# Two PSUM banks in turn instead of one for the broadcast of the q and k norms

## What is computed

```
xn  = layernorm(x)                                  # x: 4 x 4096 x 1024, f32
qkv = xn @ w_qkv;  q, k, v of 16 heads of 64
qn  = q / max(norm(q), 1e-12);  kn = k / max(norm(k), 1e-12)
att = softmax(qn @ kn.T * exp(min(logit_scale, log 100))) @ v;   att @ w_out + b_out
ffn = relu(xn @ quant(W1).T + b1) @ quant(W2).T + b2  # quant: to -1, 0, 1
out = x + attention(xn) + ffn(xn)
```

## Time and profile before

| | us |
|---|---|
| runs of the kernel before | 7316.56 and 7632.47 |
| their median | 7474.52 |
| the profiled execution, its own time | 7146.77 |
| its span (slowest core, core 2), first to last instruction | 7144.7 |
| spans of all cores | 7095.8 to 7144.7 |
| mean granted TensorE clock of the cores | 0.902 to 0.905 |
| TensorE busy with matmuls | 5821.0 (81%) |
| ScalarE busy | 2882.6 (40%) |
| VectorE busy | 2340.2 (33%) |
| mean DMA rate over the span | 78 GB/s |

### The profile page before, as it was taken

The page is one execution under the profiler, slowest core; times in us unless marked ns, Lnnn a source line. Parts: engine busy times, 40 slices in busy tenths (PEclk is TensorE's granted clock), DMA queues, the critical chain, the costliest instruction groups (busy, mean ns, idle before and its releaser), DMA issues.

```text
span 7144.7 us, 70041 instructions; the slowest of 8 cores (7095.8 to 7144.7 us)
## 1 busy us (share of the span) xinstructions
PE 5821.0 (81%) x23681; PEld 2005.4 (28%) x24072; DVE 2340.2 (33%) x2493; ACT 2882.6 (40%) x3080; POOL 21.4 (0%) x44
## 2 busy tenths in 40 slices
PE   0577877888587898889888989899999887878888
PEld 0222322333121222222222222222222244444444
DVE  2333333333254443444444444334334300000000
ACT  0011110111165576667666766667667611111111
POOL 0000000000000000000000000000000000000000
PEclk9877887888798898999989989999999999999999
DMA  5324432333412201110111011110110065555555
GB/s 180 123 73 154 133 102 72 100 126 121 111 44 68 52 11 37 34 34 11 37 34 34 14 34 23 21 19 3 21 21 1 18 168 160 154 163 159 150 156 149
DMA packets 695061, 558.43 MB, mean 78 GB/s; under 512 B 415028, under 2 KB 587188, under 8 KB 690630
## 3 DMA queue, kind: packets, MB, share of 16 engines
q10 hardware_dynamic: 540800, 306.25, 17.6%
q1 hardware_dynamic: 148166, 214.13, 9.9%
q0 software_dynamic: 5760, 33.56, 1.4%
HBM read 461.57 MB, written 92.27 MB: 78 GB/s over the span
## 4 chain that ended last, share of the span: by engine, by line
PE 71%; DMA 10%; DVE 8%; issue 4%; ACT 3%; ACTq 3%; SPq 0%; DVEq 0%; POOLq 0%
PE ps_x L807 9%; PE ps_av L799 7%; PE ps_av L803 6%; PE ps_x L810 6%; PE ps_wa L1015 3%; PE ps_wb L1015 3%; ACTq L66 3%; PE ps_wc L1075 3%; DMA wob_l<-woscr 3%; PE ps_wa L485 3%; PE ps_wb L485 3%; PE ps_wa L834 2%; PE ps_wb L834 2%; PE ps_wa L837 2%; PE ps_wb L837 2%
## 5 line engine op out<-in xcount | busy, mean ns | idle before, releaser
L854 DVE SCALAR_TENSOR_TENSOR alo<-a,ahi 128x1024 bf16<-128x1024 f32 x1024 | 1253.1, 1225 | 1832.3 <-ACT a L848 1832.3
L799 PE MATMUL ps_av<-ahi,vpk 128*128 128x512 bf16 x1930 | 766.7, 397 | 242.7 <-DVE alo L854 242.1
L803 PE MATMUL ps_av<-alo,vpk 128*128 128x512 bf16 x2048 | 803.5, 392 | 15.5 <-issue 11.1
L810 PE MATMUL ps_x<-alo,onesb 128*1 128x512 bf16 x2048 | 792.8, 387 | 0.0
L807 PE MATMUL ps_x<-ahi,onesb 128*1 128x512 bf16 x2048 | 791.3, 386 | 0.0
L845 ACT ACTIVATE ahi<-ps_wa,nscols,scols 128x1024 bf16<-128x1024 f32 x384 | 460.7, 1200 | 368.9 <-PE ps_wa L837 199.2
L845 ACT ACTIVATE ahi<-ps_wb,nscols,scols 128x1024 bf16<-128x1024 f32 x384 | 461.1, 1201 | 208.1 <-PE ps_wb L837 201.9
L1025 ACT ACTIVATE hh_sb<-ps_wa,b1cs 128x256 bf16<-128x256 f32 x128 | 60.7, 474 | 988.9 <-PE ps_wa L1015 986.7
L848 ACT ACTIVATE a<-ps_wb,nscols,scols 128x1024 f32<-128x1024 f32 x384 | 459.0, 1195 | 0.0
L848 ACT ACTIVATE a<-ps_wa,nscols,scols 128x1024 f32<-128x1024 f32 x384 | 458.5, 1194 | 0.0
L799 PEld LDWEIGHTS ps_av<-ahi,vpk 128*128 128x128 bf16 x2048 | 200.0, 98 | 904.4 <-issue 809.7
(11 more groups left out here) (189 smaller groups left out, 7680.8 us busy)
## 6 DMA issues: line engine op xcount, KB each, us to landing
wq1b<-wq1s ACTq DMA_DIRECT2D x256, 256.0 KB, 3.4
wq2b<-wq2s ACTq DMA_DIRECT2D x256, 256.0 KB, 2.7
wbh<-wscr_hi SPq DMA_DIRECT2D x40, 1024.0 KB, 6.5
wbl<-wscr_lo SPq DMA_DIRECT2D x40, 1024.0 KB, 9.7
wob_h<-woscr ACTq DMA_DIRECT2D x128, 256.0 KB, 2.7
wob_l<-woscr ACTq DMA_DIRECT2D x128, 256.0 KB, 3.1
wt<-W1T POOLq DMA_DIRECT2D x8, 2048.0 KB, 9.8
xt<-xT SPq DMA_DIRECT2D x8, 2048.0 KB, 17.8
```

The source lines that it names most:

```text
L799: em.do("t", lambda e, kt=kt, pr=pr, ah=ah, bh=bh: e.matmul(ps_av[:], vpk[bh][:, kt * 128:(kt + 1) * 128], ahi[pr][:, ah * 512:(ah + 1) * ...
L803: em.do("t", lambda e, kt=kt, pr=pr, ah=ah, bh=bh: e.matmul(ps_av[:], vpk[bh][:, kt * 128:(kt + 1) * 128], alo[pr][:, ah * 512:(ah + 1) * ...
L810: em.do("t", lambda e, kt=kt, pr=pr, ah=ah: e.matmul(ps_x[0:1, :], onesb[:], alo[pr][:, ah * 512:(ah + 1) * 512], start=False, stop=(kt == ...
L854: em.do("v", lambda e, pr=pr: e.scalar_tensor_tensor(out=alo[pr][:], in0=a32[pr][:], scalar=1.0, in1=ahi[pr][:], op0=ALU.mult, op1=ALU.sub ...
```

## The change

The broadcasts of `qk_normalize` alternate between two PSUM banks: even steps use `ps_x`, odd steps `ps_av`, for q and for k alike. There is one count per bank (`rn_ck`), which lives through all chunks: the broadcast of step t waits for the mul that last read its bank, that is mul t-2, instead of mul t-1. At the end of every `qk_normalize` both counts that `header` waits for are set to the larger of the two, that is to the last mul. No instruction is added or removed, and no DMA is moved; only the waits and the PSUM addresses differ.

```diff
-            ck_last = 0
+            rn_b = [ps_x[:, 0:CH], ps_av[:, 0:CH]]
             for t in range(8):
                 pb = t % 2
-                em.wait("t", "v", max(ck_rn, ck_rnps[0]))
-                em.do("t", lambda e, t=t, rn_ps=rn_ps: e.matmul(rn_ps, Ft(t), nrmall[:, 0:CH],
-                                                                start=True, stop=True), inc="t")
+                em.wait("t", "v", max(ck_rn, rn_ck[pb]))
+                em.do("t", lambda e, t=t, pb=pb: e.matmul(rn_b[pb], Ft(t), nrmall[:, 0:CH],
+                                                          start=True, stop=True), inc="t")
                 ckt = em.cnt["t"]
                 em.wait("v", "t", ckt)
                 em.wait("v", "dstg", ck_kstg_sp)
                 em.selfw("v")
-                em.do("v", lambda e, t=t, pb=pb, pbase=pbase, rn_ps=rn_ps: e.tensor_mul(
+                em.do("v", lambda e, t=t, pb=pb, pbase=pbase: e.tensor_mul(
                     out=t1b2[pb][:], in0=p32[(pbase + t) % 12][:],
-                    in1=rn_ps), inc="v")
+                    in1=rn_b[pb]), inc="v")
                 ckv = em.cnt["v"]
-                ck_rnps[0] = ckv
+                rn_ck[pb] = ckv
...
+            ck_rnbcq_v = max(rn_ck)
+            ck_psav_v = max(rn_ck)
...
-        rnps_q = [0]
-        rnps_k = [0]
+        rn_ck = [0, 0]
...
-                             ps_x[0:16, 0:CH], 0, ck_ss_q, ps_x[:, 0:CH], rnps_q)
-                ck_rnbcq_v = rnps_q[0]
+                             ps_x[0:16, 0:CH], 0, ck_ss_q, None, None)
...
-                             ps_wc[0:16, 512:1024], 1, ck_ss_k, ps_av[:, 0:CH], rnps_k)
-                ck_psav_v = rnps_k[0]
+                             ps_wc[0:16, 512:1024], 1, ck_ss_k, None, None)
```

## The result

Some executions of either kernel run 1.5 to 10% longer with a lower granted clock on one die; the ratio below leaves them out.

The account below looks back on a forecast made before the run. TensorE bounds the kernel, idling in phase A for qk_normalize's mul (182.1 us). Early departures 39.5, headers 10.5 and clock 2.5 sum to 52.5 us: 7146.77 to 7094.3, given as 7422.0 on the runs' median scale; range 7088 to 7580.

Parts of the forecast that it names:

- The sum: Whole kernel: 39.5 + 10.5 + 2.5 = 52.5 us less, 0.73%.
- The short step: Steps of a normalize without a landing wait: 3.12 to 2.37 us, gain 0.75 us, 4 times in a normalize.
- The early departure: TensorE leaves the normalize after chunks 0 to 3 (q) and 7 (k) 7.89 us earlier: 39.5 us in five places.
- The cover of 3 us: Behind a q-normalize: VectorE's first square is ready 3 us before TensorE asks for it, despite VectorE's lag.
- rival 2: Behind the q-normalize: a late landing exceeds the cover, 1.6 us lost in each of 4 places, 7101; chance 0.04.
- The header: After the k-normalize of chunks 0 to 6: sums wait for the last mul, gain 1.85 us each, 1.5 after clock loss.
- The late starts of chunks 1 to 3: TensorE's waits at those chunks' starts, 19.0 us: VectorE is behind because the header held it; they move along.
- The clock: TensorE's clock: 0.35 us lost per header after idling; 0.5 us gained in each of five places behind broadcasts 6 and 7.
- Rivals 1 and 3: Header sums at lower clock: 1, 4.5 us instead of 0.35, 7123, chance 0.08; 3, all 32 records, 7170, chance 0.03.
- rival 5: Normalize and work behind: clock stays at 2.4 GHz, nearly all 182.1 us come back, 6997; chance 0.03.
- What a measurement can tell: Whole kernel: about 2%, 143 us, can be told from no change; chance of an outcome within that 0.92.
- Rival 4: Normalize: the landing sets the pace, the second bank buys nothing, VectorE eats TensorE's early end, no effect, 7147; chance 0.07.

Follow-up runs that it names:

- q alone: The changed kernel with two banks only in the q-normalize, the k-normalize on its old bank: phase A 1609.3 us, ratio 0.9940 to the kernel before.
- e4: The changed kernel plus a TensorE wait for the last mul at the end of each normalize: phase A 1623.6 us, ratio 0.9997 to the kernel before.
- k alone: The changed kernel with two banks only in the k-normalize, the q-normalize on its old bank: phase A 1621.0 us, no ratio.
- e6_stg_one_bank: The kernel before, still with one bank, but two pairs of staging tiles and a semaphore for each: phase A 1557.1 us, ratio 0.9905.

## Why the prediction was right, and where it was not

The mechanism and its sum came out. What failed is the last step, from the sum to the time: "The median of the runs shown is 7474.52, 4.6% above the profiled execution; on its scale it is 7422.0. I give that as the time", and with it the 2% that a measurement of this kernel was said to be able to tell from no change.

- *The sum.* 52.5 us were forecast; phase A got 54.4 us shorter on like cores and 55.7 over all, the span 59.4 between the slowest cores and 50.8 between the medians, and the ratio says 0.78% where 0.73% was given. That it came this close is partly luck: two small terms were both wrong and cancel (see the clock), and some 2.5 us come from shorter waits for the first squares.
- *The short step.* 2.37 us forecast, 2.36 measured, decided by VectorE's own chain. Right.
- *The early departure.* 7.89 us in each of five places: confirmed at the places themselves (51.2 - 10.8 = 40.4 us in five, where 39.5 were forecast), by q alone (7.8 us each) and by the run in which TensorE stays (35 us lost, 30.3 of them as waits in the five places). It is the largest term, and e4 shows that it isn't to be had from the short steps. The cover of 3 us over VectorE's lag was 4 us here; no wait appeared, so rival 2 fell.
- *The header.* 1.85 us instead of 7.89, because the joined count makes its sums wait for mul 7. Right: the wait stands in the profile (41.8 us, 7 times), and k alone gave 22.3 us where 7 x 1.85 + 7.89 = 20.8. Read at the places, a header gave 1.5 us, as 1.85 - 0.35 had it. The late starts of chunks 1 to 3, though, do not hang on the header as the prediction says: VectorE is behind there because of the landings of v. ScalarE waited 81.5 us for them between 480 and 1200 us on a core with late starts (core 2, before) and 64.8 us on one nearly without (core 6), and with a second v buffer the late starts are gone.
- *The clock.* Both small terms were too large. I had put down a loss of 0.35 us per header. The 128 records took 73.5 us on the mean of eight cores and 72.9 before, and on the four like cores 73.8 and 72.4: 0.1 to 0.2 us per header, inside the spread of the cores. I had put down a gain of 0.5 us for the tiles behind broadcasts 6 and 7; in chunk 0 the clock rose 2.5 us after the tile's first matmul (388.57 to 391.11), no sooner than before (from about 389.8 to 392.36), and over the four q-normalizes the stretch from the tile's start to the second L462 got 0.1 us shorter each. The -2.5 and +2.5 us cancel in the sum. Rivals 1 and 3, with 4.2 and 11.2 us more in each header, did not come true, nor did rival 5, with 150 us or more.
- *What a measurement can tell.* This step failed. I had written that about 2% can be told from no change, and so expected the outcome to pass as none (0.92). The interval came out at 0.9897 to 0.9948, a quarter of a percent on either side, and a gain of 0.78% stands clear of 1. The 4.3% between the two runs shown were not the scatter of comparable executions; such ones agree much better. Not always as well as here: the intervals of e4_stay and e6_stg_one_bank are 0.6 and 0.8% on either side.
- *The time itself.* 7422.0 us was put on the scale of a median of two runs. The kernel before has a median of 7291.91 over ten, so the figure given was above it, although a gain was forecast; the median after is 7190.96. The step that failed is the choice of scale, a median of two runs that lie 4.3% apart, which carries their scatter, almost six times the gain that was forecast. The profiled execution's own time less the sum, 7094.3, lies 7.4 us from the 7086.94 that the profiled execution took. The range, 7088 to 7580, holds the median after, mostly because it is 6.7% wide; the profiled execution lies 1 us below its lower end, which the terms alone had set.
- *Rival 4* (the landing sets the pace, and the second bank buys nothing) fell with the change itself, and with it went the page "TensorE: Matmul & The Clock Gate" of the Trainium skill, section "HAM oscillation — how this bites in real kernels", as a guide to this case: it tells of another kernel, for which PSUM double-buffering gave no further gain. Here it gave 54.4 us, and 58.5 once the landing wait was gone.

## What to carry to other kernels

A second buffer can give more than the steps it shortens: ask what stands behind the last step on the in-order engine, for the largest part of the gain here (35 of 54.4 us) was that TensorE could leave while VectorE still waited for a DMA. The same question finds the places where it gives little, here a coarse count that lets the next stage wait for the last reader of either bank. And where one loop has two waits in turn, look at both: the staging alone brought 86.2 us, the bank alone 54.4, both together 144.7. For the forecast: put a change worth 1% on the time of executions that can be compared, not on the median of two that differ by 4.3%.

## What the runs showed of the hardware

- The cores of one execution fall into two groups in phase A, 1643 and 1664 us before, 1589 and 1606 us after, by the wait for v's landings; in the run with a second v buffer all eight lie within 6.3 us.
- Behind the reciprocal, f32 broadcasts in a row start 1.70 to 1.84 us apart (365.75, 367.59, 369.29 and 371.11 us, core 0 of the changed kernel), while one alone takes 2.04 us.
- An engine that issues DMAs delays its own next instruction: in the run with two banks and two staging pairs ScalarE's two issues per pair of steps (the second takes 0.49 us) made the steps from mul 2 to 3, 4 to 5 and 6 to 7 2.55 us instead of 2.36.
